# Destination rows of edges: TensorE spreads them from SBUF into PSUM, in place of broadcast loads from DRAM

## What is computed

```python
q = x @ Wq + bq; k = x @ Wk + bk; v = x @ Wv + bv
e = edge_attr @ We
kj = k[src] + e
alpha = jnp.sum(q[dst] * kj, axis=-1) / jnp.sqrt(jnp.float32(D))
amax = jax.ops.segment_max(alpha, dst, num_segments=N)
p = jnp.exp(alpha - amax[dst])
denom = jax.ops.segment_sum(p, dst, num_segments=N)
w = p / denom[dst]
msg = (v[src] + e) * w[:, None]
agg = jax.ops.segment_sum(msg, dst, num_segments=N)
return agg + x @ Ws + bs
```

## Time and profile before

| | us |
|---|---|
| median of 3 runs | 5613.62 |
| lowest and highest | 5603.17, 5616.82 |
| the profiled execution, its own time | 5620.39 |
| its span, first to last instruction | 5618.6 |
| layers 0, 1 and 2 in the span, about | 110 to 1510, 1560 to 2980, 3030 to 4510 |

### The profile page before, as it was taken

The page is one execution under the profiler, slowest core; times in us unless marked ns, Lnnn a source line. Parts: engine busy times, 40 slices in busy tenths (PEclk is TensorE's granted clock), DMA queues, the critical chain, the costliest instruction groups (busy, mean ns, idle before and its releaser), DMA issues. The chain is left out here.

```text
span 5618.6 us, 110747 instructions
## 1 busy us (share of the span) xinstructions
PE 3767.4 (67%) x23392; PEld 3052.9 (54%) x23392; DVE 3430.9 (61%) x14010; ACT 1712.7 (30%) x3613; POOL 2346.3 (42%) x2436
## 2 busy tenths in 40 slices
PE   3377666666616666666664377777777659999566
PEld 2255554445514555454454267666666659999322
DVE  6366666665705666666673266666666743334799
ACT  1233334443214333444331233333332120000266
POOL 6455555555062565555523455555555030000000
PEclk9576778887856777888785666776776759999688
DMA  2233333433122333443322233333333040000000
GB/s 66 64 81 83 82 91 97 104 99 86 29 69 63 84 83 83 102 103 100 94 62 48 62 78 79 80 80 78 78 78 74 19 165 2 2 2 2 1 3 4
DMA packets 552464, 373.24 MB, mean 66 GB/s; under 512 B 399872, under 2 KB 476768, under 8 KB 551839
## 3 DMA queue, kind: packets, MB, share of 16 engines
q1 hardware_dynamic: 353919, 144.08, 9.9%
q10 hardware_dynamic: 121536, 142.57, 8.3%
q0 software_dynamic: 76384, 79.48, 7.9%
HBM read 300.59 MB, written 65.24 MB: 65 GB/s over the span
## 5 line engine op out<-in xcount | busy, mean ns | idle before, releaser
L236 POOL DMA_INDIRECT arena<-node_table,arena x1564 | 1508.3, 964 | 1194.0 <-SPq L736 744.5
L874 PE MATMUL ps<-arena 128*128 x4980 | 1085.9, 354 | 458.4 <-issue 155.6
L1003 DVE SCALAR_TENSOR_TENSOR arena<-ps,arena 128x129 f32<-128x129 f32 x2490 | 633.4, 289 | 1082.7 <-issue 514.1
L874 PEld LDWEIGHTS ps<-arena 128*128 128x128 f32 x4980 | 883.1, 249 | 610.1 <-issue 605.8
L236 POOL DMA_INDIRECT arena<-last_node_table,arena x782 | 743.8, 951 | 637.8 <-SPq L736 406.9
L1034 DVE TENSOR_SCALAR arena<-arena 128x128 f32<-128x128 uint16 x2490 | 878.0, 357 | 169.3 <-PE ps L874 59.8
L861 PE MATMUL ps<-arena 128*128 x2496 | 555.6, 359 | 197.8 <-issue 154.9
L861 PE MATMUL ps<-arena,e 128*128 x2484 | 564.9, 366 | 157.3 <-issue 96.6
L861 PEld LDWEIGHTS ps<-arena 128*128 128x128 f32 x2496 | 449.0, 249 | 296.8 <-issue 293.2
L861 PEld LDWEIGHTS ps<-arena,e 128*128 128x128 f32 x2484 | 463.3, 256 | 248.2 <-issue 245.0
L1321 PE MATMUL ps<-arena 128*128 128x192 bf16 x6875 | 585.2, 246 | 13.0 <-DVEq L1481 5.3
(11 more groups left out here) (351 smaller groups left out, 4253.9 us busy)
## 6 DMA issues: line engine op xcount, KB each, us to landing
arena<-in_attr SPq DMA_DIRECT2D x1173, 96.0 KB
arena<-slot_rows ACTq DMA_DIRECT2D x249, 320.0 KB
edge_counts<-al ACTq DMA_DIRECT2D x397, 100.0 KB
arena<-node_table,arena POOLq DMA_INDIRECT x1564
edge_counts<-stage ACTq DMA_DIRECT2D x198, 100.0 KB
arena<-last_node_table,arena POOLq DMA_INDIRECT x782
arena<-edge_counts SPq DMA_DIRECT2D x24, 500.0 KB, 5.6
stage<-edge_counts SPq DMA_DIRECT2D x16, 500.0 KB
```

Of the source, the lines that this page charges most:

```text
L236: pool.indirect_dma_start(out=RING[:, t % R_SLOTS, XO:XO + n], out_offset=None, in_=table[:, :], in_offset=bass.IndirectOffsetOnAxis(ap=ID ...
L874: ins = pe.matmul(BPS[j % 2][:, 0:AB], WOH[j % 2][:, q], RINGS[:, bass.ds(r, 1), q, D32:D32 + AB].rearrange("p o f -> p (o f)"), start=q = ...
L1003: ins = dve.scalar_tensor_tensor(PR[j % 3][:, q], UPS[j % 2][:, q * AB:(q + 1) * AB], 1.0, row, ALU.mult, ALU.mult, accum_out=AL[w % 2][:, ...
```

## The change

`DB` moves from the scratch memory of the first phase to memory that lasts. The DRAM table, its four stores and all broadcast loads go. In their place PE has `spread_rows(m)` for the batches 2m and 2m+1: for each of the four slots one bf16 matmul whose weights are one column of the identity matrix, repeated 128 times, so that every partition of the result holds the slot's row of `DB`. The result is float32 in one bank of PSUM (columns 2560 to 3071), 256 columns for each of the two batches. ACT's Square reads it there. PE waits for `sq`, Square of both earlier batches, before it writes the bank again, and releases `rows`; ACT waits for `rows`. PE spreads the first four batches ahead of the loop, then in every even step j the batches j+4 and j+5, after `expand(j+1)`. The old name `RPS`, two rows of the softmax in another bank, becomes `RPE`.

```diff
@@ in build
-    row_t = nc.dram_tensor("slot_rows", (ROWS, P), bf16).ap()
...
+        DB = V(mem.take(NWIN * P // 2), NWIN, P, dt=bf16)
...
-                sp.wait_ge(s["row"], 1)
-                sp.dma_start(row_t[0:WIN_T0[8], :].rearrange("(w p) e -> p w e", w=8), DB[0:WMAX, 0:8]).then_inc(s["wr"], 16)
-                for w in range(8, NWIN):
-                    sp.dma_start(row_t[WIN_T0[w]:WIN_T0[w] + WIN_N[w], :], DB[0:WIN_N[w], w]).then_inc(s["wr"], 16)
                 sp.wait_ge(s["ldw"], 16 * 9)
-                sp.wait_ge(s["wr"], 16 * 8)
+                sp.wait_ge(s["wr"], 16 * 4)
...
-            ROWB = [V(rowb + q * 5 * BT * P // 2, 5 * BT * P, dt=bf16) for q in range(2)]
+            RPS = [ps[:, 2560 + BT * P * k:2560 + BT * P * (k + 1)] for k in range(2)]
...
-                    for r in range(2):
-                        act.dma_start(ROWB[r], row_t[5 * BT * r:5 * BT * (r + 1), :].rearrange("(o t) e -> o (t e)", o=1)
-                                      .to_broadcast([P, 5 * BT * P])).then_inc(rwl[r], 16)
-                    def load_rows(r):
-
-                        act.dma_start(ROWB[r % 2], row_t[5 * BT * r:5 * BT * (r + 1), :].rearrange("(o t) e -> o (t e)", o=1)
-                                      .to_broadcast([P, 5 * BT * P])).then_inc(rwl[r % 2], 16)
-
                     def one_hot_rows(j):
 
-                        r = j // 5
-                        act.wait_ge(rwl[r % 2], 16 * (r // 2 + 1))
+                        act.wait_ge(s["rows"], j // 2 + 1)
                         if j >= 6:
                             act.wait_ge(s["pu"], j - 5)
                         o = OHT[j % 6]
-                        act.activation(o, ROWB[r % 2][:, (j % 5) * BT * P:(j % 5 + 1) * BT * P], ACT.Square, bias=pid1, scale=-1.0)\
-                            .then_inc(s["sq"], 1)
+                        act.activation(o, RPS[j % 2], ACT.Square, bias=pid1, scale=-1.0).then_inc(s["sq"], 1)
                         act.wait_ge(s["sq"], j + 1)
                         act.activation(o, o, ACT.Relu, bias=1.0, scale=-1.0).then_inc(s["oht"], 1)
-                        if j % 5 == 4 and r + 2 < NBAT // 5:
-                            load_rows(r + 2)
...
+                    def spread_rows(m):
+
+                        if m:
+                            pe.wait_ge(s["sq"], 2 * m)
+                        for j in range(2 * m, min(2 * m + 2, NBAT)):
+                            w = window_of(j)
+                            n, c = WIN_N[w], BT * j - WIN_T0[w]
+                            for q in range(BT):
+                                ins = pe.matmul(RPS[j % 2][:, q * P:(q + 1) * P], identb[0:n, c + q:c + q + 1].to_broadcast([n, P]),
+                                                DB[0:n, w], start=True, stop=True)
+                        ins.then_inc(s["rows"], 1)
+
...
+                    spread_rows(0)
+                    spread_rows(1)
                     expand(0, block_of(0))
                     for w in range(NWIN + 1):
                         for ja, jb in steps(w):
                             for j in ja:
                                 if j + 1 < NBAT:
                                     expand(j + 1, block_of(j + 1))
+                                if j % 2 == 0 and j + 4 < NBAT:
+                                    spread_rows(j // 2 + 2)
                             for j in jb:
                                 aggregate(j)
```

More of the change, by code:

```diff
@@ L273, in build @@
         tmp = Words(layer_mem + EARLY * BT * RW, LOW + 3225, (u_mem, u_end))
-        with phase(nc, "qp ldd ldx ldw lds cst cio cnt gi ms p1 p2 p3 c1 c2 c3 mm mc st var std h row tr key ktr kc xs wr ends ht hc up uc") as (block, s):
+        with phase(nc, "qp ldd ldx ldw lds cst cio cnt gi ms p1 p2 p3 c1 c2 c3 mm mc st var std h tr key ktr kc xs wr ends ht hc up uc") as (block, s):
             FD = V(tmp.take(NG), NG, dt=i32)
@@ L291, in build @@
             DZ = V(tmp.take(NWIN * P), NWIN, P)
-            DB = V(tmp.take(NWIN * P // 2), NWIN, P, dt=bf16)
             D4 = V(tmp.take(NQ * G4 * P), NQ, G4 * P, dt=i32)
@@ L585, in _ @@
                 st.link(dve.tensor_copy(DB, DZ))
-                dve.sem_inc(s["row"], 1)
                 dve.tensor_scalar(MK, DZ, 0.5, -BIG, ALU.is_lt, ALU.mult)
@@ L680, in conv @@
             o = small.take(2 * P)
-            RPS = ps[0:1, o:o + 2 * P].rearrange("p (a b) -> p a b", b=P)
+            RPE = ps[0:1, o:o + 2 * P].rearrange("p (a b) -> p a b", b=P)
             o = small.take(3)
@@ L704, in conv @@
             names = " ".join(f"eld{k}" for k in range(LOADS))
-            names += " free landed rwl0 rwl1 st ast pst ht hc up uc sq oht pu pr woh bmm add oh hm turned scanned ends chained spread rescale shifted expd pturned weights"
+            names += " free landed rows st ast pst ht hc up uc sq oht pu pr woh bmm add oh hm turned scanned ends chained spread rescale shifted expd pturned weights"
             names += " ah am acp kst nd skb at atc no yd hn xst deg root var std"
@@ L708, in conv @@
                 eld = [s[f"eld{k}"] for k in range(LOADS)]
-                rwl = [s[f"rwl{k}"] for k in range(2)]
                 @block.gpsimd
@@ L932, in _ @@
                         pe.wait_ge(s["scanned"], w + 1)
-                        pe.matmul(RPS[:, 0, 0:n], FW[0:n, P - 1:P], identf[0:n, 0:n], start=True, stop=True)
-                        pe.matmul(RPS[:, 1, 0:n], MX[0:n, 0:1], identf[0:n, 0:n], start=True, stop=True).then_inc(s["ends"], 1)
+                        pe.matmul(RPE[:, 0, 0:n], FW[0:n, P - 1:P], identf[0:n, 0:n], start=True, stop=True)
+                        pe.matmul(RPE[:, 1, 0:n], MX[0:n, 0:1], identf[0:n, 0:n], start=True, stop=True).then_inc(s["ends"], 1)
                         pe.wait_ge(s["chained"], w + 1)
@@ L1061, in softmax @@
                         dve.wait_ge(s["ends"], w + 1)
-                        dve.tensor_tensor_scan(out=cf[:, 1:n + 1], data0=CFD[:, t0:t0 + n], data1=RPS[:, 0, 0:n],
+                        dve.tensor_tensor_scan(out=cf[:, 1:n + 1], data0=CFD[:, t0:t0 + n], data1=RPE[:, 0, 0:n],
                                                initial=cf[:, 0:1], op0=ALU.add, op1=ALU.max)
                         st.link(dve.tensor_tensor_scan(out=CBX[:, 0:n][:, ::-1], data0=CBD[:, t0:t0 + n][:, ::-1],
-                                                       data1=RPS[:, 1, 0:n][:, ::-1], initial=-BIG, op0=ALU.add, op1=ALU.max))
+                                                       data1=RPE[:, 1, 0:n][:, ::-1], initial=-BIG, op0=ALU.add, op1=ALU.max))
                         if w:
```

## The result

| | before | after |
|---|---|---|
| median, us | 5613.62 | 5724.19 |
| lowest and highest, us | 5603.17, 5616.82 | 5698.09, 5730.64 |
| the profiled execution, own time and span, us | 5620.39, 5618.6 | 5698.09, 5695.9 |

The change makes the kernel slower: ratio 1.019, interval 1.0173 to 1.0208, or 110 us by the medians. The forecast was 5810, so its direction held and its size was too large: 196 us instead of 110.

The account below looks back on a forecast made before the run. Bound by engines waiting for one another, with PE's releases seen late under gathers, no engine full. Terms -5 + 100 + 99 + 0 = +194 gave 5810 us; range 5500 to 6000, likeliest case 5700 to 5920.

Parts of the forecast that it names:

- What bounds the kernel: Gather loop: engines wait for one another, none full; PE's releases are seen up to 13 us late while gathers are issued.
- L: Lateness with which ACT sees PE's spread release in even steps: taken as 1.2 us, between 0.04 and 2.5.
- Removed loads, starts -5: Row-load waits at the starts of three layers go: 5 us saved, 0 to 20 possible.
- PE's matmuls, +100: 2490 added spread matmuls on PE, 249 us of work, cost +100 us; bounds nothing and 249.
- share of 0.4: Part of PE's added time on the path, from two three-window stretches: 37.4 us more work, 14 to 15 us longer.
- The coupling, +99: Even steps: ACT's copy and PE's window counts wait behind spread and one-hot; 199 us, half on the path, bounds 0 and 385.
- rival 1: Loads made PE's releases late; removing them saves 227 us, so the kernel is faster at 5483 us; chance 0.22.
- about 2 us per pair of steps: Sign of a right forecast: growth of windows of layers 0 and 1 from the fifth on, more than windows 1 to 3.
- PE's wait for Square, 0: PE's spread waits for Square of batch j+3, computed a step before; costed at nothing.
- Releases against loads, 0: Extra spread releases, up to +172 us, set off against fewer DMAs saving 56 to 227 us: 0, from -227 to +172.
- 2: Rival: everything finds cover, no change; PE +33, coupling +25, loads -56, giving 5616 us; chance 0.08.
- 3: Rival: PE's releases queue during gathers, 172 us on top of the forecast, 5980 us; chance 0.2.

Follow-up runs that it names:

- e3: Kernel before with the spread's matmuls added on PE, without wait or release, result unread, loads kept: 4640.38 us, ratio 1.0058.
- e6: Changed kernel with broadcast loads, waits and releases kept, but each spread in the odd step before: 5705.11 us, ratio 1.0058 to the kernel before.
- e4: Changed kernel with broadcast loads kept; PE spreads, both waits and the release stay, Square reads the loaded rows: 4750.69 us, ratio 1.0292 to the kernel before.
- e5: Changed kernel with ACT's order turned, copy of the counts ahead of the one-hot: 5688.28 us, ratio 1.0031 to the kernel before.
- e10: Changed kernel with each spread one step earlier, behind the aggregate, in late executions: 5694.75 against 5662.74 us for the kernel before, ratio 1.0068.
- e1: Changed kernel with each spread one step earlier, behind the aggregate, first run, in prompt executions: ratio 0.9878 to the kernel before.
- r1: Kernel before, unchanged, repeated for its trace: 5658.55 us (its median over the comparison 5670.4).
- r2: Changed kernel, unchanged, repeated beside the kernel before: 5779.33 us, ratio 1.019.
- e7: Changed kernel with each spread one step earlier, behind the aggregate, run again in prompt executions: ratio 0.9917 to the kernel before.
- e9: Either the change with earlier spread and copy first (0.9915), or the kernel before without later row loads, repeated (0.9882); the text doesn't say which.

## Why the prediction was right or wrong

**What bounds the kernel.** Right for the executions it was read from: loops between engines with late releases in them, no full engine. That these releases are late was taken as given by the kernel; the experiments show that it isn't (last section). And two of the latenesses were read off wrong pairs of rows. Counted from the start of the layer, the product at 140.83 is that of batch 3 and waits for the expansion of batch 3, the Square at 140.57 is that of batch 9 and waits for the same one; the expansion that ends at 127.67 is that of batch 4. The product at 1037.63 is that of batch 282, and 1036.47 ends the expansion of batch 283. The expansions that these products need, from the trace of before:

```profile
119.87 1.21 PE L861 MATMUL ps<-arena,e 128*128 x4
...
1031.73 0.70 PE L861 MATMUL ps<-arena 128*128 x4
```

They end at 121.08 and 1032.43. So the release in the first window was seen 19.5 us late and not 13, and the 1.2 us that I took for L is no lateness of a release.

**Removed loads, starts -5.** The first expansion is at 112.9 instead of 115.8 us: 3 us in layer 0.

**PE's matmuls, +100: the term that was mis-sized.** They sum to 293.6 us in this trace, a little above the 210 to 290 named, but their price is 27 us where measured alone (e3) and 33 with waits and releases (e6, 0.58% of 5670, up to 44 by its interval). The wrong step is the share of 0.4: measured, it is a tenth. I took it from two stretches, of layers 0 and 2, that differ by 37 us in PE's work but also in which work it is; the length went with something else. The 249 us were no time added to PE either: with its records overlapping, PE's total rose by 142 us. In after, windows 1 to 3 got 267 matmuls more and became shorter, where I foretold 4 us more for each. There the loads are gone, too, and the granted clock is 0.77 against 0.72, but with the loads kept (e6) these windows are no longer than before either. So the share there is nothing that shows beside the 6 us by which two traces of the kernel before differ in them (419.6 and 425.5).

**The coupling, +99: right in mechanism, and in size partly by luck.** The distance in even steps came out as forecast, 2.74 us for 2.7, or 154 x 1.39 = 214 us where I had 199. But L, taken as 1.2 from the wrong pair, was 0.90 us on average between the end of the spread and Square in the even steps from batch 196 on, and 0.04 in the median one. The half on the path had another reason, too, than DVE's work in hand: the odd steps gave back 152 x 0.51 = 78 us. And the price doesn't follow L: in prompt executions, where L is 0.16, I would have had 154 x 0.3 = 46 us (rival 1), and e4 against e3 gave 110.

Idle time before the window counts grew by 172.6 us; windows 4 to 10 of layers 0 and 1 grew by 83 us; undoing the coupling by ACT's order alone gave back 91 us (e5), by an earlier spread 1.2% or some 69 (e10). In windows 4 to 7 of layer 0 the length grew by 24.4 us, and the wait there from 67.4 to 126.0 us: a share on the path of 0.42, where I took half. The sign that I named beside it was wrong: "about 2 us per pair of steps". A window of 45 batches from the fifth on grew by 3 to 13 us, 7 on average, 0.3 us per pair; my own sum, 99 us over 154 steps, would have said 0.6. The tail windows of layers 0 and 1, which I expected to stay, grew by 6 to 8 us (the one of 30 batches) and 3 to 4 us (those of 15 and 10): they, too, have counts in nearly every step.

**PE's wait for Square, 0.** In after, PE is idle before the spread for 40.3 us that Square ended, of 146.4. Near enough to nothing for this placement, and not for the earlier one (105.6 us in e10).

**Releases against loads, 0.** The set-off came out right, as two terms near nothing and not as two that cancel: nothing of either is seen in late executions (e6 to e10: 1.0058 and 1.0068, loads kept and gone). In prompt ones the loads are worth 1.2%. The releases' 172 us are nowhere. I had written that by the Trainium skill ("TensorE: Matmul & The Clock Gate", "The cost: per-tile semaphore tail"), with 26 ns for each increment, this last term would be nothing. No cost of the releases shows in e6, which agrees; but the page states this of the matmuls of several tiles of the array that each increment a semaphore, and no run here has those. What it would make of L (nothing as well) fits the prompt executions alone, where a release is seen 0.04 us behind the matmul (last section).

**The sum** with the measured terms: -3, +27 to +33 for PE's matmuls, +69 to +91 for the coupling, 0: 93 to 121 us, against 110 measured. The terms are differences between these same kernels, so that the sum comes out is no proof by itself. The forecast was 86 us too high: some 70 of that are PE's matmuls. **Rivals:** 1 (5483) needed the loads to be what makes releases late; they are late without them in after, e5 and e10. 2 (cover everywhere) fell by the window counts. 3 (5980) fell by e6.

## What to carry to other kernels

When a new wait lets an in-order engine stand for a neighbour, count what is queued behind the waiting instruction and who needs that: here a copy that didn't depend on the new data stood behind it, and letting it go first took the loss from 1.9% to 0.3%. And before two rows of a timeline are read as release and waiter, count both from the start of the layer: two pairs read from the earlier trace rows were wrong here. A share of "work on the path" read from two stretches of different layers isn't a price for added work; take it from stretches that differ in that work alone, or add the work by itself. Measure a placement in all conditions in which the kernel runs: the earlier spread was 1% faster than before in one and 0.7% slower in the other.

## What the runs showed of the hardware

The same kernel took 4566 us (e1) and 5695 us (e10). First window of layer 0 in both, the same work of PE, DVE and ACT, e1 and then e10:

```profile
113.10:198.70 85.60, 61.40 (x413) 44.97 (x413) 58.07 (x325) 47.88 (x109) 64.86 (x69) 0.86 0.40 96
```

```profile
112.70:297.60 184.90, 63.46 (x413) 46.02 (x413) 57.27 (x325) 47.79 (x109) 79.98 (x85) 0.63 0.21 50
```

PE is busy for 61.4 and 63.5 us, DVE for 58.1 and 57.3: the engines' work is equal, and the waiting makes 99 us. The granted clock is lower in the longer one, but PE's busy time hardly differs. The same Square, that of batch 6, shows it. In e1 the gathers run, and ACT starts 0.04 us after the end of its spread at 118.52:

```profile
117.89 0.63 PE L844 MATMUL ps<-arena,identz 90*128 90x128 bf16 x4
...
118.56 0.47 ACT L752 ACTIVATE arena<-ps,arena 128x256 f32<-128x256 f32 x1 [1.15 <-PE ps L844]
118.64 0.94 POOL L236 DMA_INDIRECT arena<-node_table,arena  x1 [0.30 <-issue]
```

In e10, with gathers at the same spacing of 1.25 us, the spread ends at 118.38, and the Square starts 10.1 us and eight gathers later:

```profile
117.75 0.63 PE L844 MATMUL ps<-arena,identz 90*128 90x128 bf16 x4
...
127.25 0.94 POOL L236 DMA_INDIRECT arena<-node_table,arena  x1 [0.30 <-issue]
...
128.49 0.47 ACT L752 ACTIVATE arena<-ps,arena 128x256 f32<-128x256 f32 x1 [11.46 <-remote]
```

So releases late by microseconds under gathers are no property of the kernel or of the gathers alone. Where e10 gathers nothing the kinds don't differ: windows 9 and 10 of layer 0 together take 86 us in both traces, and the phases behind the layers 1133.6 us. What decides between the two kinds stays open: no experiment here controlled it. It isn't the number of the chip: chip 7 was prompt in e1 to e4 and late in r1, r2, e5 and e6, chip 4 prompt in e7 to e9 and late in e10. The change itself wasn't run in a prompt execution; e4 (1.029) is the nearest to it there, with the loads on top.

One small thing beside: Square reads its 256 columns from PSUM as float32 in 471 ns, and read them from SBUF as bf16 in 502 ns. The new source made ACT cheaper by 41 us in all (the two forms of L752, 1245 x 33 ns on average). Type and memory changed together, so no run says which of them did it, nor whether any of it was on the path.
